# A four-stage transformer block on one core: decay exponents made by TensorE, and the last pass's mask added there

## The chip, the core and the metric

The kernel runs on one core of a Trainium2 chip. A core has five engines that run side by side, each through its own list of instructions in order: TensorE (PE in the profile; its weight loads are PEld), VectorE (DVE), ScalarE (ACT), GpSimd (POOL), and SyncE (SP), which here only issues DMAs. They wait for each other by semaphores. SBUF is the on-chip memory of 128 partitions, PSUM the accumulators that TensorE writes, in banks of 512 f32 columns. The metric is the device time of one execution in microseconds.

## The reference, cut to what matters

Input x has 128 sequences of 64 tokens of 128 values (8192 tokens), ctx the same. Four layers are applied with residuals:

```python
x = x + tanh(g_xattn[0]) * mlstm(layernorm(x), ctx, ctx, gates..., rms_scale)      # 4 heads of 32
x = x + tanh(g_ffn[0])   * switch_ffn(layernorm(x), wg, w1, b1, w2, b2)            # 8 experts, top 1
x = x + tanh(g_xattn[1]) * attention(layernorm(x), ctx, ctx, mask, W1, b1, W2, b2) # 1 head, 64x64 mask
x = x + tanh(g_ffn[1])   * (layernorm(x) @ CB.T * SCB / 127 + bias)

# mlstm, per sequence and head
cs    = concatenate([0, cumsum(log_sigmoid(fg))])
log_d = where(lower_triangle, (cs - cs.T)[1:, 1:] + ig.T, very_negative)
m     = max(log_d, axis=-1)                 # a running maximum over the tokens
d     = exp(log_d - m)                      # the decays
c     = q @ k.T / sqrt(32) * d
h     = c / (max(sum(c), exp(-m)) + eps) @ v

# attention
p     = softmax(q @ k.T / sqrt(128) + mask)
```

With a_j = ig_j - (the forget sum up to j), the exponent of a decay is a_j - M_i for j <= i and very negative otherwise, where M_i is the running maximum of a up to i.

## The kernel before, in words

The tokens are worked on in 16 groups of 512 (8 sequences; 4 tiles of 128 tokens, t = 0 to 3). The program has a first pass over the 16 groups (mLSTM, second layer norm, routing, scatter to the experts' slots in DRAM), an experts' stage (16 blocks of 512 slots), and a last pass over the 16 groups (gather, attention, last product, store).

Both passes are software pipelines written out by hand: in step k each engine does stage one of group k, stage two of group k-1, stage three of group k-2 and stage four of group k-3. `over_groups` unrolls the first and last steps and puts the middle in a loop of two steps. The order on each engine within a step is the order of calls in its `first_pass` or `last_pass`; no scheduler moves anything. In the first pass the stages are:

- one: layer norm of x, context and queries turned by PE (L889, L896), gate values from keys and queries (gate_products, L908 and L909);
- two: log of the forget gates, their sums (L915), a, turned by PE (L919), the running maxima by a scan on DVE (L1198), turned back (L923), and the decays;
- three: scores (L932), scores times decays (DVE L1210), head values (L945), RMS norm;
- four: second layer norm, turned rows (turn_routed, L953), logits (L962), the choice of an expert (DVE L1267 to L1279), the count of tokens by expert (count_tokens, L972 to L976).

The decays take this way: the scan leaves 16 rows (tile and head) of 128 maxima in SBUF (mrow). SP writes them to DRAM (spread_max, m_scratch), waits for that, and reads them back broadcast to all partitions (mb, two DMAs). POOL subtracts them from a (L619) and adds the triangle's mask (cap, L624), each over 128x1024, and ACT takes exp in SBUF (L733). The scores of all four tiles lie in the four PSUM banks of `heads`, with the head values behind them in the same banks.

A few filler products, keep_clock (L882), stand in PE's list. ACT's stage-one copy of the turned queries (L707, s_qt) is what the gate products wait for. In the last pass DVE scales the scores and adds the mask (L1408), takes the maximum (L1412) and subtracts it (L1415); then ACT takes one exp over 128x256 (L822), and PE turns the result (L1087). POOL runs the gathers (L669, four for each group) and adds a bias (L676).

## Time and profile before

| | us |
|---|---|
| median of 3 runs | 669.56 |
| lowest and highest | 668.75, 670.59 |
| the profiled execution's own time | 669.89 |
| its span, first to last instruction | 668.1 |

| engine | busy us | share of the span |
|---|---|---|
| PE | 500.9 | 75% |
| DVE | 396.4 | 59% |
| POOL | 296.6 | 44% |
| ACT | 294.6 | 44% |

The mean granted clock of TensorE is 0.771 of its full 2.4 GHz; it has two levels, 0.5 and 1.0. The first pass lasts until about 358 us, the experts' stage until about 497, and the last pass until the end. The shares are means over three stages that have different limits, so a change in one stage is to be read in that stage.

### The profile page before, as it was taken

To read this page: it belongs to the slowest core of one execution; us is meant where nothing else is said; L and a number is where in the kernel's file an instruction comes from. 1 tells how busy PE (TensorE), PEld (TensorE's weight loads), DVE (VectorE), ACT (ScalarE), POOL (GpSimd) and SP (SyncE) were. 2 spreads that over 40 slices of the span, in tenths; PEclk is the share of its full clock that TensorE was granted. 3 is DMA by queue.
4 is the path that set the end of the run, shared out by engine and by line. 5 is a ranking of instruction groups with operands and counts; after the bars stand their busy time and mean duration, and the time that the engine had idled before them with its cause. 6 is when DMAs were issued, how large, how long until landed. Compare 5 with 4: busy or idle time off the path is not lost. (4 is left out here: it accounts for less than half of the span.)

```text
span 668.1 us, 12708 instructions
## 1 busy us (share of the span) xinstructions
PE 500.9 (75%) x3659; PEld 364.5 (55%) x3659; DVE 396.4 (59%) x1536; ACT 294.6 (44%) x674; POOL 296.6 (44%) x249
## 2 busy tenths in 40 slices
PE   0637798888887888787644899999951777777685
PEld 0525676666666765566433477777740445444453
DVE  4115577777777777777662223232312699898883
ACT  3425445544444445354211333433322566666673
POOL 2024455556655555555644000000008888888720
PEclk9996657666556667556665799999995797999996
DMA  6943333222333332132501233343224445455521
GB/s 142 189 105 80 80 97 97 79 66 61 90 91 87 95 95 79 32 86 57 142 18 38 58 94 95 104 117 94 80 76 70 86 93 128 96 121 124 134 84 47
DMA packets 87362, 60.26 MB, mean 90 GB/s; under 512 B 7811, under 2 KB 79142, under 8 KB 87334
## 3 DMA queue, kind: packets, MB, share of 16 engines
q1 hardware_dynamic: 76070, 51.48, 29.5%
q0 software_dynamic: 11264, 8.43, 7.3%
q8 instruction: 14, 0.23, 0.1%
q14 instruction: 14, 0.11, 0.1%
HBM read 34.46 MB, written 17.04 MB: 77 GB/s over the span
## 5 line engine op out<-in xcount | busy, mean ns | idle before, releaser
L669 POOL DMA_INDIRECT s_xs<-slots_y,s_gidx x64 | 98.9, 1545 | 152.4 <-DMA slots_y<-s_ye 134.8
L619 POOL TENSOR_TENSOR s_ex<-s_am,s_mb 128x1024 f32<-128x1024 f32 x16 | 30.3, 1896 | 146.6 <-DMA s_mb<-m_scratch 146.6
L147 ACT ACTIVATE s_xn<-s_xs,s_ln_shift,s_ln_rstd 128x128 f32 (+1 forms) x192 | 77.6, 481 | 22.6 <-DVE s_ln_shift L140 21.8
L797 ACT ACTIVATE s_ht<-heads,s_cols 128x512 f32<-128x512 f32 x64 | 44.0, 687 | 85.2 <-PE heads L1026 84.9
L99 DVE BATCH_NORM_STATS2 s_ln_stats<-s_xs 128x6 f32 (+1 forms) x256 | 54.4, 279 | 30.7 <-DMA s_xs<-slots_y,s_gidx 19.1
L645 POOL DMA_INDIRECT slots_x<-s_xn,s_sidx x64 | 63.0, 984 | 18.2 <-issue 17.2
L1026 PE MATMUL heads<-s_xet,s_w_sb 128*128 128x512 f32 x128 | 60.5, 617 | 1.7 <-DVE s_xet L1373 1.7
L1033 PE MATMUL bank<-s_w_sb,s_ht 128*128 128x128 f32 x512 | 59.9, 275 | 0.9 <-DVE s_ye L1382 0.9
L1033 PEld LDWEIGHTS bank<-s_w_sb,s_ht 128*128 128x128 f32 x512 | 58.5, 192 | 1.5 <-issue 1.5
L932 PE MATMUL heads<-s_ht,s_kt 128*64 128x256 f32 x256 | 57.9, 602 | 0.0
L733 ACT ACTIVATE s_ex<-s_ex 128x1024 f32<-128x1024 f32 x16 | 16.9, 1057 | 80.2 <-POOL s_ex L624 80.2
L945 PE MATMUL heads<-s_vaug,s_cw 64*64 64x33 f32 x1024 | 42.8, 233 | 5.7 <-issue 5.4
L945 PEld LDWEIGHTS heads<-s_vaug,s_cw 64*64 64x64 f32 x1024 | 38.1, 149 | 13.4 <-issue 13.0
L908 PE MATMUL bank<-s_kc,s_kt 128*128 128x8 f32 x128 | 36.6, 360 | 4.5 <-ACT s_qt L707 3.9
L1382 DVE TENSOR_TENSOR s_ye<-bank,s_b2b 128x512 f32<-128x512 f32 x16 | 11.1, 692 | 47.3 <-PE bank L1033 47.3
L1373 DVE COPY s_xet<-bank 128x512 f32<-128x512 f32 x16 | 11.1, 692 | 47.1 <-PE bank L1019 47.1
L1026 PEld LDWEIGHTS heads<-s_xet,s_w_sb 128*128 128x128 f32 x128 | 24.2, 199 | 26.9 <-issue 24.3
L624 POOL TENSOR_TENSOR s_ex<-s_ex,s_cap 128x1024 f32<-128x1024 f32 x16 | 37.5, 2345 | 1.9
L716 ACT ACTIVATE s_ht<-bank 32x512 f32<-32x512 f32 x64 | 37.3, 583 | 1.2
L908 PEld LDWEIGHTS bank<-s_kc,s_kt 128*128 128x128 f32 x128 | 34.2, 328 | 6.5 <-issue 5.5
L909 PE MATMUL bank<-s_kqkv,s_qt 128*128 128x8 f32 x128 | 36.8, 361 | 0.0
L676 POOL TENSOR_TENSOR s_ex<-s_xs,s_fbias 128x512 f32<-128x512 f32 x16 | 27.4, 1711 | 19.2 <-DVE s_xs L1428 19.2
(169 smaller groups left out, 1008.7 us busy)
## 6 DMA issues: line engine op xcount, KB each, us to landing
s_mb<-m_scratch SPq DMA_DIRECT2D x32, 256.0 KB, 4.0
slots_x<-s_xe SPq DMA_DIRECT2D x8, 516.0 KB, 11.3
s_xe<-slots_x SPq DMA_DIRECT2D x16, 258.0 KB, 3.2
s_xs<-in_x_dram SPq DMA_DIRECT2D x16, 256.0 KB, 4.0
s_ctxb<-in_ctx_dram SPq DMA_DIRECT2D x16, 256.0 KB, 2.9
s_kpt<-s_kt SPq DMA_DIRECT2D x16, 256.0 KB, 4.0
s_w_sb<-in_L_ffn_w_dram SPq DMA_DIRECT2D x16, 256.0 KB, 3.2
slots_y<-s_ye SPq DMA_DIRECT2D x16, 256.0 KB, 2.3
```

The costliest lines, as they stand in the source:

```text
L99: last = dve.bn_stats(self.stats[:, i * GT + t, :], tile(t))
L147: last = act.activation(out(t), tile(t), ACT.Identity, bias=self.shift[:, j:j + 1], scale=self.rstd[:, j:j + 1])
L624: pool.tensor_tensor(ex[:, q, :].rearrange("p (r i) -> p r i", i=S), ex[:, q, :].rearrange("p (r i) -> p r i", i=S), cap[:, :].unsqueeze(1 ...
L645: pool.indirect_dma_start(out=slots_x, out_offset=bass.IndirectOffsetOnAxis(ap=sidx[:, q, t:t + 1], axis=0), in_=xn2[:, q, t, :], in_offse ...
L669: pool.indirect_dma_start(out=xs[:, n * D:(n + 1) * D], out_offset=None, in_=slots_y, in_offset=bass.IndirectOffsetOnAxis(ap=gidx[:, n:n + ...
L716: act.activation(qbd[hp, q, :].rearrange("p (b h i) -> p b h i", b=BG, h=NH)[:, :, h, :], bank[0][hp, :].rearrange("p (b i) -> p b i", b=B ...
L797: act.activation(ht[:, s_par, c, :], heads[:, c, :], ACT.Gelu_apprx_tanh, bias=col).then_inc(h_done, 1)
L908: pe.matmul(tile, kt[:, q, t * P:(t + 1) * P], kc[:, :], start=True, stop=False)
L932: last = pe.matmul(heads[(b % 2) * S:(b % 2 + 1) * S, t, 0:NH * S], kt[:, q, b * S:(b + 1) * S], qbd[:, q, b * NH * S:(b + 1) * NH * S], s ...
L945: last = pe.matmul(heads[bp, t, NH * S + h * HA:NH * S + (h + 1) * HA], cw[bp, t, h, :], vaug[bp, q, t, h, :], start=True, stop=True)
L1026: pe.matmul(heads[:, c, :], w1_sb[:, wq, c * P:(c + 1) * P], xet[:, :], start=True, stop=True).then_inc(h_ps, 1)
L1033: last = pe.matmul(bank[6][:, t * D:(t + 1) * D], ht[:, q, c, t * P:(t + 1) * P], w2_sb[:, wq, c, :], start=(c == 0), stop=(c == FC - 1))
```

## The change

Decays: mrow's two halves (the two sequences of a tile) now go straight from SBUF to two rows (partitions 32 and 33) of a right-hand tile dec_r, with two DMAs and no trip through DRAM. DVE copies the turned a to the first 16 rows of a left-hand tile dec_l. The other rows hold constants: selectors of ones for the 16 rows, -1 for the two rows of maxima, and an identity against the triangle's mask. One product of dec_l by dec_r per half, into two banks of `heads`, is the exponent, and ACT takes exp from PSUM. POOL's two passes are gone. The scores now use those two banks (two tiles each) and the head values the other two, so DVE multiplies scores by decays in two instructions in place of four, and scales the heads in one in place of four. On ACT the copy of the queries is called behind the decays and the routing's exp.

Last pass: a scaled mask is added by a product with the identity behind the scores. DVE takes the maximum from PSUM and scales it, and ACT takes exp from PSUM with the maximum as bias, in four instructions of 64 columns. POOL and DVE build the constant tiles at the start, ahead of the point at which PE and DVE begin their first pass.

```diff
             def spread_max(g, half, q):
                 hold(sp, mrow_done, g + 1, consts)
-                sp.dma_start(m_dram[q].rearrange("b (r i) -> r b i", i=S),
-                             mrow[:, q, :].rearrange("r (b i) -> r b i", b=2)).then_inc(m_out[q], 16)
-                hold(sp, m_out[q], half * 16 + 16, consts)
-                hold(sp, l_done, g - 1, consts)
+                hold(sp, l_ps, g - 1, consts)
                 for b in range(2):
-                    sp.dma_start(mb[b * S:(b + 1) * S, q, :],
-                                 m_dram[q][b:b + 1, :].to_broadcast([S, R * S])).then_inc(m_in[q], 16)
+                    sp.dma_start(dec_r[32 + b:33 + b, q, :], mrow[:, q, b * S:(b + 1) * S]).then_inc(m_in[q], 16)
...
+            pool.wait_ge(cleared, 4)
+            step(pool.memset(dec_r[0:R, :, :], 1.0))
+            for q in range(2):
+                step(pool.affine_select(out=dec_r[0:R, q, :], in_=dec_r[0:R, q, :], compare_op=ALU.is_equal, fill=0.0, base=0,
+                                        pattern=[[1, R], [0, S]], channel_multiplier=-1))
+            step(pool.tensor_copy(dec_r[S:P, :, :].rearrange("p q (r i) -> p (q r) i", i=S),
+                                  cap[S:P, :].unsqueeze(1).to_broadcast([S, 2 * R, S])))
+            step(pool.tensor_copy(dec_l[S:P, :, :].rearrange("p q (b i) -> p (q b) i", i=S),
+                                  ident[S:P, S:P].unsqueeze(1).to_broadcast([S, 4, S])))
...
-            def exponents(g, half, q):
...
-                pool.tensor_tensor(ex..., am..., mb..., ALU.subtract).then_inc(l_done, 1)
...
-                pool.tensor_tensor(ex..., ex..., cap..., ALU.add).then_inc(lcap_done, 1)
...
             def decays(g, half, q):
-                act.wait_ge(lcap_done, g + 1)
-                act.activation(ex[:, q, :], ex[:, q, :], ACT.Exp).then_inc(ex_done, 1)
+                act.wait_ge(l_ps, g + 1)
+                need(act, cw_done, nth(g - 2, 1, 2))
+                act.activation(ex[:, q, :], heads[:, 0:2, :].rearrange("p u n -> p (u n)"), ACT.Exp).then_inc(ex_done, 1)
...
                 if two:
                     values(*two)
-                if one:
-                    queries(*one)
                 if two:
                     decays(*two)
                 if four:
                     routed_exp(*four)
                 if one:
+                    queries(*one)
                     soft_part(*one)
                     queries_by_head(*one)
...
             def probabilities(g, half, q):
-                act.wait_ge(sm_steps, nth(g, 3, 3))
+                act.wait_ge(sm_steps, nth(g, 2, 2))
                 need(act, prt_ps, g)
-                act.activation(pr[:, :, :], sm[:, 1, :, :], ACT.Exp).then_inc(pr_done, 1)
+                for t in range(GT):
+                    last = act.activation(pr[:, t, :], heads[:, 0, t * S:(t + 1) * S], ACT.Exp, bias=smx[:, 1, t:t + 1],
+                                          scale=float(D) ** -0.5)
+                last.then_inc(pr_done, 1)
...
+            def decay_exponents(g, half, q):
+
+                pe.wait_ge(arow_done, g + 1)
+                hold(pe, m_in[q], half * 32 + 32, consts)
+                need(pe, cw_done, nth(g - 1, 2, 2))
+                for u in range(2):
+                    last = pe.matmul(heads[:, u, :], dec_l[:, q, :], dec_r[:, q, u * GW:(u + 1) * GW], start=True, stop=True)
+                last.then_inc(l_ps, 1)
...
             def running_max(g, half, q):
                 dve.wait_ge(at_ps, g + 1)
+                need(dve, l_ps, g - 1)
+                dve.tensor_copy(dec_l[0:R, q, :], bank[6][0:R, 128:256]).then_inc(arow_done, 1)
...
-            def exponents3(g, half, q):
+            def score_maxima(g, half, q):
...
-                dve.scalar_tensor_tensor(out=sm..., in0=heads..., scalar=float(D) ** -0.5, in1=mask..., op0=ALU.mult, op1=ALU.add)
...
+                dve.tensor_reduce(smx[:, 0, :], heads[:, 0, 0:GT * S].rearrange("p (c k) -> p c k", k=S), AX, ALU.max).then_inc(sm_steps, 1)
...
-                dve.tensor_tensor(sm..., sm..., smx..., ALU.subtract).then_inc(sm_steps, 1)
+                dve.tensor_scalar(smx[:, 1, :], smx[:, 0, :], -(float(D) ** -0.5), None, ALU.mult).then_inc(sm_steps, 1)
```

The scores of the last pass (scores3) get the product with the identity behind them:

```diff
+                pe.matmul(heads[:, 0, 0:GT * S], ident[:, :], mask_s[:, :].unsqueeze(1).to_broadcast([P, GT, S]),
+                          start=False, stop=True).then_inc(s3_ps, 1)
```

On PE, in a full step of the first pass, before, from the end of the head values to the first gate products (L953 is turn_routed, L896 turn_queries, L962 the logits, L908 and L909 the gate products):

```order
L945 MATMUL heads<-s_vaug,s_cw 64x33 x7
L953 MATMUL bank<-s_ident,s_xn 128x128 [waits ln12_applied1]
L953 MATMUL bank<-s_ident,s_xn 128x128 x3
L896 MATMUL bank<-s_ident,s_xn 128x128 [waits qbd_done,ln12_applied0]
L896 MATMUL bank<-s_ident,s_xn 128x128 x3
L962 MATMUL bank<-s_wg_sb,s_xt 128x8 [waits xt2_done,late_in]
L962 MATMUL bank<-s_wg_sb,s_xt 128x8 x3
L908 MATMUL bank<-s_kc,s_kt 128x8 [waits qt_done,mtok_done,kt_done]
```

The same place now (L961 is turn_routed, L928 the new product, L893 turn_queries, L970 the logits, L905 the first gate product):

```order
L961 MATMUL bank<-s_ident,s_xn 128x128 [waits cum_used]
L961 MATMUL bank<-s_ident,s_xn 128x128 x3
L37 ISA [waits arow_done]
L928 MATMUL heads<-s_dec_r,s_dec_l 128x512 [waits cw_done,m_in1,consts]
L928 MATMUL heads<-s_dec_r,s_dec_l 128x512
L890 REGISTER_ALU
L29 REGISTER_ALU [waits ln12_applied0]
L893 MATMUL bank<-s_ident,s_xn 128x128 [waits qbd_done]
L893 MATMUL bank<-s_ident,s_xn 128x128 x3
L970 MATMUL bank<-s_wg_sb,s_xt 128x8 [waits xt2_done]
L970 MATMUL bank<-s_wg_sb,s_xt 128x8 x3
L905 MATMUL bank<-s_kc,s_kt 128x8 [waits mtok_done,qt_done,consts,kt_done]
```

Two 128x512 products have come between the turned rows and the turned queries; the order around them is as it was.

On ACT, in a full step, before, from the copy of the values (L702) to the four copies of the queries by head (L716):

```order
L702 ACTIVATE s_vaug<-s_ctxb 128x16x32 [waits pv_done]
L707 ACTIVATE s_qt<-bank 128x512 [waits xt1_done]
L733 ACTIVATE s_ex<-s_ex 128x1024 [waits lcap_done]
L753 ISA
L29 ISA [waits route]
L755 ACTIVATE s_spread<-s_below 128x32 [waits weight_done]
L721 ISA
L722 ACTIVATE s_eneg<-s_negabs 128x16 [waits gate_steps]
L723 ISA
L724 ACTIVATE s_softp<-s_eneg 128x16 [waits gate_act]
L716 ACTIVATE s_ht<-bank 32x8x64 x4
```

The same place now (L696 copies the values, L728 is the decays' exp, L750 the routing's, L701 the queries' copy):

```order
L696 ACTIVATE s_vaug<-s_ctxb 128x16x32 [waits pv_done]
L29 ISA [waits l_ps]
L728 ACTIVATE s_ex<-heads 128x1024 [waits cw_done]
L748 ISA
L29 ISA [waits route]
L750 ACTIVATE s_spread<-s_below 128x32 [waits weight_done]
L701 ACTIVATE s_qt<-bank 128x512 [waits xt1_done]
L715 ISA
L716 ACTIVATE s_eneg<-s_negabs 128x16 [waits gate_steps]
L717 ISA
L718 ACTIVATE s_softp<-s_eneg 128x16 [waits gate_act]
L710 ACTIVATE s_ht<-bank 32x8x64 x4
```

The copy of the queries has moved from ahead of the decays' exp to behind the routing's.

## Rows read from the trace of the kernel before

**Rows 1.** Busy time by window: start:end and length, each engine, clock, DMA.

```profile
core 0: us, PE busy (x) PEld busy (x) DVE busy (x) ACT busy (x) POOL busy (x), PEclk, DMA share, GB/s
60.00:318.00 258.00, 219.34 (x1707) 167.17 (x1708) 190.61 (x765) 122.61 (x293) 143.37 (x119) 0.62 0.28 78
376.00:499.00 123.00, 116.95 (x695) 86.42 (x693) 34.57 (x62) 43.88 (x63) 0.00 (x0) 1.00 0.32 88
```

**Rows 2.** Waits: who for whom, us in total, times, longest.

```profile
PE bank L972 <- DVE s_onehot L1279: 18.7, 15, 3.5
```

**Rows 3.** Timeline of one step: start us, us, engine line, operation [idle before].

```profile
167.60 0.69 PE L953 MATMUL bank<-s_ident,s_xn 128*128 128x128 f32 x4 [1.23 <-DVE s_xn L154]
...
169.20 1.85 PE L962 MATMUL bank<-s_wg_sb,s_xt 128*128 128x8 f32 x8
...
170.56 0.58 ACT L707 ACTIVATE s_qt<-bank 128x512 f32<-128x512 f32 x1
...
171.29 0.56 PE L908 MATMUL bank<-s_kc,s_kt 128*128 128x8 f32 x2 [0.23 <-ACT s_qt L707]
...
173.35 2.34 POOL L624 TENSOR_TENSOR s_ex<-s_ex,s_cap 128x1024 f32<-128x1024 f32 x1
...
173.60 2.13 DVE L1279 TENSOR_TENSOR s_onehot<-s_first_best,s_choice 128x32 bf16<-128x32 f32 x1
...
174.26 0.57 PE L909 MATMUL bank<-s_kqkv,s_qt 128*128 128x8 f32 x2
...
175.80 0.21 PE L972 MATMUL bank<-s_onehot,s_tri_b 128*128 128x40 bf16 x1 [0.96 <-DVE s_onehot L1279]
...
176.60 1.98 PE L932 MATMUL heads<-s_ht,s_kt 128*64 128x256 f32 x8
```

**Rows 4.** Busy time by window, three short stretches of that step.

```profile
160.11:161.08 0.97, 0.97 (x7) 0.74 (x8) 0.85 (x4) 0.95 (x2) 0.67 (x2) 0.50 0.18 64
...
162.05:163.02 0.97, 0.97 (x21) 0.75 (x20) 0.81 (x9) 0.00 (x0) 0.86 (x1) 1.00 0.20 68
...
168.84:169.81 0.97, 0.97 (x6) 0.80 (x5) 0.70 (x2) 0.49 (x2) 0.00 (x0) 0.50 0.93 224
```

**Rows 5.** Timeline of the experts' stage, L1026 at its start and later.

```profile
370.78 6.41 PE L1026 MATMUL heads<-s_xet,s_w_sb 128*128 128x512 f32 x8 [0.94 <-DVE s_xet L1373]
...
400.85 3.60 PE L1026 MATMUL heads<-s_xet,s_w_sb 128*128 128x512 f32 x8
```

**Rows 6.** The scan in the timeline; the page's DMA issues, last number us to landing.

```profile
163.78 0.41 DVE L1198 TENSOR_TENSOR_SCAN s_mrow<-s_reset,bank 16x128 f32<-16x128 f32 x1 [0.76 <-PE bank L919]
...
s_mb<-m_scratch SPq DMA_DIRECT2D x32, 256.0 KB, 4.0
```

**Rows 7.** Timeline of the last step of the first pass, logits to exponential.

```profile
354.05 1.87 PE L962 MATMUL bank<-s_wg_sb,s_xt 128*128 128x8 f32 x8 [0.69 <-ACT s_xt L750]
...
356.41 0.23 ACT L755 ACTIVATE s_spread<-s_below 128x32 f32<-128x32 f32 x1 [2.42 <-DVE s_below L1270]
```

**Rows 8.** Timeline, PE: a wait for logf, and the last three waits for onehot.

```profile
83.81 0.61 PE L915 MATMUL bank<-s_logf,s_tri 128*128 128x16 f32 x2 [2.12 <-DVE s_logf L1184]
...
330.75 0.22 PE L972 MATMUL bank<-s_onehot,s_tri_b 128*128 128x40 bf16 x1 [3.39 <-DVE s_onehot L1279]
...
346.91 0.21 PE L972 MATMUL bank<-s_onehot,s_tri_b 128*128 128x40 bf16 x1 [2.99 <-DVE s_onehot L1279]
...
357.11 0.21 PE L972 MATMUL bank<-s_onehot,s_tri_b 128*128 128x40 bf16 x1 [1.19 <-DVE s_onehot L1279]
```

**Rows 9.** Timeline of the start.

```profile
6.41 1.11 PE L889 MATMUL bank<-s_ident,s_ctxb 128*128 128x128 f32 x4 [6.41 <-POOL s_carry L611]
...
12.54 0.86 DVE L99 BATCH_NORM_STATS2 s_ln_stats<-s_xs 128x6 f32<-128x128 f32 x4
...
31.16 0.59 SPq L465 DMA_DIRECT2D m_scratch<-s_mrow  x1
...
47.95 0.61 PE L915 MATMUL bank<-s_logf,s_tri 128*128 128x16 f32 x2 [10.31 <-DVE s_logf L1184]
```

**Rows 10.** Last pass: a wait of POOL's, and DVE's masked scores (count, busy, mean ns).

```profile
POOL s_ex L676 <- DVE s_xs L1428: 19.2, 4, 5.9
...
L1408 DVE SCALAR_TENSOR_TENSOR s_sm<-heads,s_mask 128x256 f32<-128x256 f32 x14 | 5.9, 424 | 5.1 <-PE heads L1078 4.9
```

More of the change, by code:

```diff
@@ L188, in sem @@
             return ctx.enter_context(nc.semaphore(name))
-        m_dram = [nc.dram_tensor(f"m_scratch{i}", (2, R * S), F32, kind="Internal").ap() for i in range(2)]
         slots_x = nc.dram_tensor("slots_x", (E * N, D + 1), F32, kind="Internal").ap()
@@ L341, in flamingo @@
         mrow_done = sem("mrow_done")
-        m_out = [sem(f"m_out{i}") for i in range(2)]
         m_in = [sem(f"m_in{i}") for i in range(2)]
@@ L648, in first_pass @@
             def first_pass(at):
-                _, two, three, _, five = at
+                _, _, three, _, five = at
                 if five:
                     scatter(*five)
-                if two:
-                    exponents(*two)
                 if three:
@@ L938, in head_values @@
                 for t in tiles_of:
-                    hold(pe, cw_done, nth(g, t + 1, GT), consts)
+                    if t % 2 == 0:
+                        hold(pe, cw_done, nth(g, t // 2 + 1, 2), consts)
                     if t == 0:
                         pe.wait_ge(vaug_done, g + 1)
+                        need(pe, hs_done, g)
                     for h in range(NH):
@@ L1001, in first_pass @@
                     turn_routed(*four)
+                if two:
+                    decay_exponents(*two)
                 if one:
@@ L1074, in scores3 @@
                 pe.wait_ge(kpr_in[q], half * 16 + 16)
-                need(pe, sm_steps, nth(g - 1, 1, 3))
+                need(pe, pr_done, g)
                 for b in range(BG):
                     u, p, c = b // 4, b // 2 % 2, b % 2
-                    last = pe.matmul(heads[p * S:(p + 1) * S, 0, (2 * u + c) * S:(2 * u + c + 1) * S],
-                                     qp[:, q, b * S:(b + 1) * S], kpr[:, q, b * S:(b + 1) * S], start=True, stop=True)
-                last.then_inc(s3_ps, 1)
+                    pe.matmul(heads[p * S:(p + 1) * S, 0, (2 * u + c) * S:(2 * u + c + 1) * S],
+                              qp[:, q, b * S:(b + 1) * S], kpr[:, q, b * S:(b + 1) * S], start=(u == 0 and c == 0), stop=False)
+                if isinstance(g, int) and g == 0:
+                    pe.wait_ge(mask_done, 1)
+                pe.matmul(heads[:, 0, 0:GT * S], ident[:, :], mask_s[:, :].unsqueeze(1).to_broadcast([P, GT, S]),
+                          start=False, stop=True).then_inc(s3_ps, 1)
             def turn_probabilities(g, half, q):
@@ L1326, in first_pass @@
                 if three:
-                    decayed_scores(three[0], three[2], (0, 1))
+                    decayed_scores(three[0], three[2], 0)
                 if two:
@@ L1338, in first_pass @@
                 if three:
-                    decayed_scores(three[0], three[2], (2, 3))
+                    decayed_scores(three[0], three[2], 1)
                 if two:
@@ L1462, in last_pass @@
                 if three:
-                    exponents3(*three)
+                    score_maxima(*three)
                 if four:
```

91 lines of the change are left out of this document (41 added, 50 removed).

## The prediction, made before the changed kernel ran

> **What bounds the kernel now.** I read the stages first, in a table of busy time by window [rows 1]: the reader should see that in the first pass (60 to 318 us) PE is busy 219.3 of 258 us at a mean granted clock of 0.62, with DVE at 191 and POOL at 143. So the first pass belongs to PE, at mostly half clock, while the experts' stage runs at full clock. Then the waits of PE's count of tokens for DVE's onehot, 18.7 us in 15 waits [rows 2], and then one turn of the loop in order of time [rows 3]: PE goes almost without a pause from the turned rows (L953, 167.60) over the logits (L962, 169.20) and the gate products (sixteen instructions, L908 at 171.29 to L909 at 174.26, which ends at 174.83). Then it stands until 175.80, because DVE's 32-column onehot (L1279) takes 2.13 us: it ends at 175.73, just after POOL's 2.34 us L624 (175.69). PE's order is fixed, so what is put into it is paid in full unless it fills one of these pauses. The clock in the step goes 0.50, 1.00, 0.50 [rows 4]: it rises once the scores and the filler products have run and falls again under the narrow products.
>
> **Product on PE (two 128x512 f32).** Each becomes two instructions, and stands between L953 and L896 in the order. At half clock four such calls (x8) take 6.4 us from 370.78, the last of them already after the rise, and L1026 at full clock has x8 in 3.60 [rows 5]. At 1.2 GHz a call streams four times 512 columns, 1.7 us, so the pair costs 3.4 us; at 2.4 GHz 1.8. Its place, 168.3, is at 0.50 [rows 4], so 3.4 is the upper end. But 3.4 us of wide streaming resembles what stands ahead of the rise in the trace, so I expect the granted clock to rise behind it for a short while. There lie the logits (1.85) and the gate products (3.5); they are many weight loads and gain some 40%, not 50%. I take 1.2 us back, net 2.2. The lower end is 1.0 (part of the product at full clock, and the return).
>
> Is its input there? The scan of the maxima ends at 164.19, and the copy put ahead of it on DVE adds 0.2. The old broadcast took 4.0 us from issue to landing, the new transfers of 4 KB less; even with 4.0 the rows are in by 168.7 against 168.3 [rows 6]. The cost is 0 to 0.4; I take 0.1 with the copy.
>
> **The queries' copy on ACT moves behind routed_exp.** Now ACT copies the queries (L707, 0.58) at 170.56, while PE does the logits, and the gate products begin 0.24 behind the logits' end (171.05, 171.29) [rows 3]. In the new order the copy stands behind the exponential of the routing (routed_exp), which waits for DVE's first two steps on the logits. In an undisturbed place that chain is seen alone: logits end 355.92, exponential 356.41 to 356.64, so 0.72 [rows 7]. Add the copy, 0.6 with handoff, and 0.15 to PE: 1.47, less the 0.24 of now: **1.25 us more on PE in each step that has both**. Nothing lies between logits and gate products in PE's order to hide it. Zero would need the logits to be done long before, which the order excludes; 1.6 if DVE or ACT is late. Also queued behind that copy is soft_part, but it waits for the gate products anyway.
>
> **POOL's two passes over 128x1024 go.** They hold up DVE. With them gone the onehot is ready during the gate products, whose later start covers it. Of 18.7 us of waits [rows 2] the last three (3.39, 2.99, 1.19) belong to the drained end of the pass [rows 8]; 11.1 are left in 12 full steps and go. Once PE also waited 2.12 us for logf [rows 8], behind a late exponent; that goes. add_heads remains on POOL, earlier in the step, and can still stall DVE, under cover of the gate products. SP's DRAM round trip was not awaited in the middle of the pass, and its loss gives nothing more. Fewer and longer DVE instructions on PSUM and fewer waits at the head values lie in DVE's slack: 0.
>
> **Start.** POOL now builds wide constant tiles (6,144 columns in four instructions and some small ones) behind two more clears on DVE. By L624's 2.34 us for 1024 columns that is 14 us; one-input work should be cheaper, I take 10. The last constant, now at 6.4, then comes at 20 (16 to 25), and DVE's first statistics start there instead of at 12.54 [rows 9]. But SP sends the first maxima only at 31.16, behind its clearing of the slots, and PE's next forget_sums stands until 47.95 with 10.31 us of waiting [rows 9]. The delay of 8 us goes almost wholly into that wait: maxima at 34, landed at 37, product to 41, queries and gate products to 46, forget_sums at 48.6. I take +1.6 for the first two groups; ends 0 and +8.
>
> **Last pass.** The mask's product adds two instructions of 256 columns, 0.45 us at full clock; the DVE add (0.42) and the subtract over 128x256 go, a tiny multiply comes; four small exponentials replace one on ACT, about 0.7 more. While POOL gathers, it sets the pace: it waits for DVE in only 4 of its adds [rows 10]. So nothing there, and about +1 over the last steps, where ACT and PE are in the chain (-1 to +3).
>
> **Sum**, by the profiled run, 669.9 us with its surroundings for a span of 668.1, 0.3 above the median of 669.56:
> - 12 full steps x (2.2 + 1.25 + 0.1) = +42.6
> - waits that go, -11.1 - 2.1 = -13.2
> - one filling step without the stall: 3.5; start 1.6; drained end: product 3.2 against 2.2 of the 3.39: +1.0. Together +6.1
> - last pass +1.0
>
> In all +36.5, so 706.4 by the profiled run and **706 us** by the median. With the product at its lower end: 12.5 x 1.2 = 15 less, 691; at its upper end 15 more, 721.
>
> **Rivals.**
> 1. *The clock stays up through the pass, and the kernel is faster.* For it: in the experts' stage, with wide products all along, the clock is 1.00 [rows 1], and the new product comes where it is lowest. Against it: some 7 us of narrow products follow it, and the clock now falls in just such a stretch. Price: half clock covers about 11 us of PE work per step, which would give back 4.8; against the product's 1.8, 1.25 and 0.1, less 1.0 of waits, the step is 2.6 us shorter; over 12.5 steps -32, about 640. It decides from the point where the clock gives back 2.9 us per step beyond my 1.2 (36.5 over 12.5 steps). The Trainium skill, TensorE: Matmul & The Clock Gate (What's actually happening), says that the throttled state is the default and activity releases it. By that rule more activity can only help, and it speaks for this rival; by the trace the release does not last a step, which speaks for 706.
> 2. *The product is paid in full at 1.2 GHz* and the start is partly bare: 12.5 x 1.2 + 4 more, 725. For it: the product begins at 0.50 every time in the trace. Against: the rise behind each wide stretch.
> 3. *The product comes nearly free of clock cost*, the rise falls within it: about 691.
> 4. *PE isn't the bound, the stalls are.* The product would lie in the present waits: -13 and some 14 for the copy and the start, about 669, no change. Against it: PE's wait ahead of L953 is upstream of the product, and behind it only the onehot's wait is left.
>
> **Chances.** Forecast (697 to 715) 0.60; rival 3 and what lies near it, 0.15; rival 2, 0.12; rival 1, 0.07; rival 4, 0.06. A measurement of this kernel tells 0.3%, 2 us, from no change. Faster: rival 1 and a third of rival 4, 0.09; within: 0.03; slower 0.88. The range 687 to 722 leaves out rivals 1 and 4 and the far end of 2.
>
> **What would show it.** The pair of 128x512 products should take 3.4 us where the clock starts at 0.50, with a rise behind it. The first gate product should stand 1.4 us idle behind ACT's copy of the queries; count of tokens should no longer wait for the onehot, and that instruction should be 0.2 us. The step should be 21.5 to 22 us against about 19 now. The first statistics on DVE should start near 20 us, and forget_sums of the second group near 48.6. In the last pass POOL's gathers should keep their spacing. I am wrong if the mean clock of the first pass is well above 0.7, or if PE idles elsewhere and the step stays near 19.

## The result: slightly faster, where 5.5% slower was forecast

The changed kernel takes 665.26 us (median of 12 runs, 656.54 to 673.09), the kernel before 669.15 (12 runs beside them, 666.05 to 673.66). The ratio is 0.9883, 95% interval 0.9847 to 0.9919. In two later sets of runs, each beside the kernel before, it was 0.9732 (0.9682 to 0.9781) and 0.9649 (0.9582 to 0.9716). The forecast was 706, with 687 as the lower end, so it was wrong in sign. Ratios leave out executions over 1.5% above the fastest of their kernel and medians do not; below, ratios are compared.

The profiled execution took 669.75 us with a span of 668.0, at a mean granted clock of 0.830 (before: 669.89, 668.1 and 0.771). As it is one of the longer executions of the changed kernel, it shows mostly the long kind of step, and an execution with a span of 646.8 us stands beside it further down.

Busy time by window in the profile after (columns as in [rows 1]): the first pass, and its 12 full steps alone.

```profile
60.00:318.00 258.00, 214.78 (x1722) 151.06 (x1722) 152.45 (x695) 119.42 (x286) 82.38 (x87) 0.74 0.16 51
82.31:320.50 238.19, 197.08 (x1597) 138.60 (x1596) 143.18 (x648) 110.21 (x264) 79.99 (x84) 0.74 0.16 51
```

Against [rows 1] POOL's busy time fell from 143 to 82 us, DVE's from 191 to 152, and PE's from 219 to 215 although two wide products per step were added: the granted clock rose from 0.62 to 0.74. The mean full step is 19.85 us, forecast at 21.5 to 22 and 19.57 before.

What PE waited for from 60 to 318 us (us in total, times, longest us):

```profile
PE bank L905 <- ACT s_qt L701: 18.1, 13, 1.5
PE bank L961 <- DVE s_xn L154: 16.0, 13, 1.5
```

The wait for the onehot [rows 2] is gone from the full steps. The one that was forecast in its place, of the gate products for the queries' copy, has come with 1.4 us each. One step in order of time answers to [rows 3] (start us, us, engine line, operation, idle before):

```profile
175.32 0.65 PE L961 MATMUL bank<-s_ident,s_xn 128*128 128x128 f32 x4 [1.34 <-DVE s_xn L154]
175.81 1.88 PE L928 MATMUL heads<-s_dec_r,s_dec_l 128*128 128x512 f32 x4
177.52 0.60 PE L893 MATMUL bank<-s_ident,s_xn 128*128 128x128 f32 x4
177.96 0.96 PE L970 MATMUL bank<-s_wg_sb,s_xt 128*128 128x8 f32 x8
...
179.06 0.18 DVE L1282 TENSOR_REDUCE s_top<-bank 128x4 f32<-128x32 f32 x1
...
179.59 0.23 ACT L750 ACTIVATE s_spread<-s_below 128x32 f32<-128x32 f32 x1 [0.29 <-DVE s_below L1285]
179.72 0.58 ACT L701 ACTIVATE s_qt<-bank 128x512 f32<-128x512 f32 x1
180.44 0.36 PE L905 MATMUL bank<-s_kc,s_kt 128*128 128x8 f32 x2 [1.53 <-ACT s_qt L701]
...
180.96 1.16 DVE L1294 TENSOR_TENSOR s_onehot<-s_first_best,s_choice 128x32 bf16<-128x32 f32 x1
...
183.44 0.19 PE L980 MATMUL bank<-s_onehot,s_tri_b 128*128 128x40 bf16 x1
```

Read this against the forecast. The four product instructions take 1.88 us, because the clock is up here; the forecast had it down. Behind them the logits take 0.96 instead of 1.85 us. The logits end at 178.92, but DVE takes the first look at them only at 179.06, as it was still scaling the heads; then the exponential, the copy and the gate products follow, 1.52 us behind the logits. The count (183.44) no longer waits. This is one of the three full steps of the profile in which the product takes 1.88 us (18.89 us long); in the other nine it takes 3.0 to 3.6.

The start came as forecast (timeline, start us, us, engine line, operation; answers to [rows 9]):

```profile
19.25 1.12 PE L886 MATMUL bank<-s_ident,s_ctxb 128*128 128x128 f32 x4 [19.25 <-POOL s_carry L621]
...
33.13 1.25 SPq L467 DMA_DIRECT2D s_dec_r<-s_mrow  x2
...
48.30 0.45 PE L912 MATMUL bank<-s_logf,s_tri 128*128 128x16 f32 x2
```

Forecast were 20, 34 and 48.6. The first full step of the loop began at 82.31 against 78.75. The last gather of the last pass started at 632.32 against 628.40, and the last output's work at 664.50 against 664.67, so the end is 4.1 us shorter. That distance varies from one execution to the next, though: it is 32.2 us here, 34.9 in a later profile of the changed kernel, 36.3 before and 34.6 in another profile with the last pass as before.

### The profile page after: what moved, and what is told of

The parts are those of the page before. It is cut to its first block and busy times, and to the rows that moved or that the text cites. A ratio compares the mean times of both kernels' runs of the same rounds, so it can differ in the third digit from the quotient of the medians.

```text
span 668.0 us, 12750 instructions
## 1 busy us (share of the span) xinstructions
PE 508.3 (76%) x3755; PEld 353.9 (53%) x3755; DVE 349.0 (52%) x1459; ACT 301.2 (45%) x722; POOL 238.0 (36%) x225
## 5 line engine op out<-in xcount | busy, mean ns | idle before, releaser
L627 POOL TENSOR_TENSOR s_hs<-s_hs,s_head_w 128x512 f32<-128x512 f32 x16 | 20.2, 1264 | 154.4 <-DVE s_hs L1268 154.4
L928 PE MATMUL heads<-s_dec_r,s_dec_l 128*128 128x512 f32 x64 | 49.9, 927 | 5.3 <-DMA s_dec_r<-s_mrow 4.7
L953 PE MATMUL heads<-s_vaug,s_cw 64*64 64x33 f32 x1024 | 39.6, 226 | 9.1 <-issue 6.9
L905 PE MATMUL bank<-s_kc,s_kt 128*128 128x8 f32 x128 | 29.9, 306 | 21.7 <-ACT s_qt L701 21.7
L953 PEld LDWEIGHTS heads<-s_vaug,s_cw 64*64 64x64 f32 x1024 | 36.1, 141 | 15.9 <-issue 15.4
L905 PEld LDWEIGHTS bank<-s_kc,s_kt 128*128 128x128 f32 x128 | 26.6, 257 | 23.3 <-issue 23.3
L1397 DVE TENSOR_TENSOR s_ye<-bank,s_b2b 128x512 f32<-128x512 f32 x16 | 11.1, 691 | 47.3 <-PE bank L1043 47.3
L716 ACT ACTIVATE s_eneg<-s_negabs 128x16 f32<-128x16 f32 x16 | 3.5, 216 | 71.1 <-DVE s_negabs L1193 71.1
L1388 DVE COPY s_xet<-bank 128x512 f32<-128x512 f32 x16 | 11.1, 692 | 46.0 <-PE bank L1029 46.0
L1073 PE MATMUL bank<-s_ident,s_xn 128*128 128x128 f32 x64 | 11.4, 304 | 29.8 <-ACT s_xn L147 29.8
L118 ACT ACTIVATE s_ln_log<-s_ln_ve 128x8 f32<-128x8 f32 (+1 forms) x38 | 7.7, 204 | 56.6 <-DVE s_ln_ve L112 51.3
```

What stands on the lines that cost most here:

```text
L905: pe.matmul(tile, kt[:, q, t * P:(t + 1) * P], kc[:, :], start=True, stop=False)
L928: last = pe.matmul(heads[:, u, :], dec_l[:, q, :], dec_r[:, q, u * GW:(u + 1) * GW], start=True, stop=True)
L953: last = pe.matmul(heads[bp, 2 + t // 2, (t % 2 * NH + h) * HA:(t % 2 * NH + h + 1) * HA], cw[bp, t, h, :], vaug[bp, q, t, h, :], start=Tr ...
```

## The experiments

Ratios are to the kernel before, with its 95% interval; a change "on queries first" starts from the first kernel.

**Parts of the change.** First, the changed kernel with ScalarE's copy of the queries ahead of the decays' exponential, as it was, in two sets of runs:

```diff
+                if one:
+                    queries(*one)
                 if two:
                     decays(*two)
                 if four:
                     routed_exp(*four)
                 if one:
-                    queries(*one)
                     soft_part(*one)
```

> The changed kernel with ACT's copy of the queries called ahead of the decays' exp again. If that copy, waiting behind the routing's exp, costs PE 1.25 us per step as forecast (1.36 measured as L905's wait), the wait goes and the kernel gains 12 x 1.2 = 14 us against the changed one: about 0.967 of the kernel before. Rival: the pause is only moved, since the logits and the choice then hold up the count of tokens, or the clock falls sooner: within 4 us of the changed kernel, 0.985 to 0.995.

> ScalarE's copy of the queries ahead of the decays' exponential, as before. Its 1.36 us per step alone would give 12 x 1.36 = 16 us under the changed kernel of this batch. If it also brings all the steps to the kind with the product at full clock, the gain is over 16 us and no step of the profile is near 20 us.

Measured: 631.47 us, 0.9523 (0.9485 to 0.9562), and again 631.02 us, 0.9523 (0.9481 to 0.9564). In the second set the changed kernel stood at 0.9649, so the copy's place costs 0.0126, 8 us, with an interval of some 5 us to either side; by the medians (645.97) it is 15. Other readings are higher: against the changed kernel's 0.9732 in its other set it is 14 us, and by the mean full step (17.03 us here, 18.10 and 18.19 in the two later profiles of the changed kernel) 13 to 14. The forecast's 15 is at the upper end of that. My expectation for the first set, 0.967 from the result's ratio, was too cautious. My expectation that no step would be near 20 held (16.28 to 17.85).

Decays and order as changed, last pass as before (the functions probabilities, scores3 and exponents3 of the kernel before put back):

> The decays' half of the change alone, the last pass as before. Theory: the first pass is 4 to 6 us later in its end, and the last pass (4 us shorter after the last gather in the changed kernel) gets its time back: 0.995 to 1.005. Rival: the gain of 4 us in the last pass came with the phase of the clock and not with the edit: the same as the changed kernel, about 0.988.

Measured: 651.24 us, 0.9812 (0.9763 to 0.9861), faster than either of my two expectations. It differs from queries first in the copy's place and in the last pass; in this set the two together are 0.0289, 19 us. The last pass's half alone:

> The last pass's half alone, the decays as before. Theory: DVE has 0.4 to 0.7 us less per step there, it is no longer a step behind POOL's gathers, and the kernel gains about 4 us: 0.994. The forecast's term: +1 us, 1.0015. Rival: phase of the clock, 1.000.

Measured: 660.37 us, 0.9973 (0.994 to 1.0005), which is -1.8 us (-4.0 to +0.3). The last output's work started 34.8 us behind the last gather's start, within the 34.6 to 36.3 of the profiles with the last pass as before. Forecast was +1.0; whether this half gains anything is not shown.

The kernel before with the new constants, built into tiles that nothing reads (CONSTS 29, the same memsets and selects):

> The kernel before with the changed kernel's eight more constants and two more clears, built into tiles that nothing reads. The forecast's term for the start: +1.6 us (ends 0 and +8), 1.002 of the kernel before. With the whole delay of DVE's first statistics on the path, +7 us, 1.010.

Measured: 662.75 us, 0.9998 (0.9974 to 1.0022). The first full step began at 82.11, as in the changed kernel, and yet nothing of that is left at the end. Its mean full step is 19.06 us (19.57 in the profile before), so it also serves as a second profile of the old order.

The kernel before with one POOL pass over 128x1024 instead of two:

```diff
                 pool.tensor_tensor(ex...,
-                                   am[:, q, :].unsqueeze(2).to_broadcast([P, R, S]),
+                                   cap[:, :].unsqueeze(1).to_broadcast([P, R, S]),
                                    mb..., ALU.subtract).then_inc(l_done, 1)
...
-                pool.tensor_tensor(ex..., ex..., cap..., ALU.add).then_inc(lcap_done, 1)
...
-                act.wait_ge(lcap_done, g + 1)
+                act.wait_ge(l_done, g + 1)
```

> The kernel before, where POOL makes the exponents in one pass over 128x1024 instead of two (cap less maxima; the gates' part is left out, so the exponents are not the reference's). By the forecast's term, the wait of the count for DVE's onehot goes: 0.93 us in each of 12 full steps, 11 us less, 0.983 of the kernel before. If the stall of DVE by POOL costs nothing else, and the clock stands as before, no more than that. If the clock is what sets the step, 0.99 to 1.00.

Measured: 641.41 us, 0.9676 (0.9646 to 0.9705), 21 us less, where the forecast had 13.2 for both passes. What PE waited for over the 12 full steps (us in total, times, longest), first before, then with one pass:

```profile
PE bank L972 <- DVE s_onehot L1279: 11.1, 12, 3.5
PE bank L915 <- DVE s_logf L1184: 2.1, 1, 2.1
```

```profile
PE bank L968 <- DVE s_onehot L1275: 3.2, 8, 0.5
PE bank L911 <- DVE s_logf L1180: 0.4, 1, 0.4
```

DVE's three small instructions with two inputs from SBUF, over the same steps (groups, busy us and mean ns), first before, then with one pass:

```profile
L1279 DVE TENSOR_TENSOR s_onehot<-s_first_best,s_choice 128x32 bf16<-128x32 f32 x12 | 24.5, 2043 | 0.4
L1273 DVE SCALAR_TENSOR_TENSOR s_first_best<-s_below,s_prio 128x32 f32<-128x32 f32 x12 | 12.3, 1023 | 0.4
L1178 DVE SCALAR_TENSOR_TENSOR s_negabs<-s_gates 128x16 f32<-128x16 f32 x12 | 9.9, 822 | 0.4
```

```profile
L1269 DVE SCALAR_TENSOR_TENSOR s_first_best<-s_below,s_prio 128x32 f32<-128x32 f32 x12 | 17.9, 1495 | 0.4
L1275 DVE TENSOR_TENSOR s_onehot<-s_first_best,s_choice 128x32 bf16<-128x32 f32 x12 | 12.2, 1014 | 0.4
L1174 DVE SCALAR_TENSOR_TENSOR s_negabs<-s_gates 128x16 f32<-128x16 f32 x12 | 4.7, 391 | 0.4
```

Together the three fall from 3.89 to 2.90 us per step. The third is the first step of the gates; it stood beside POOL's add_heads, which ran late because it comes behind the two passes.

The wait for the onehot that is gone, 7.9 us, is less than half of the gain: the step falls from 19.57 us (19.06 in the profile with the constants) to 17.39. The rest can be read against the profile with the constants, 20 us over the 12 steps. PE stands idle 10.0 us less (36.6 to 26.6). There PE waited 8.4 us in 4 steps for DVE's logf, in a chain of lateness: POOL's second pass ends at 103.53, ACT's exponential of the decays at 104.62, the routing's exponential behind it at 104.73, and only then DVE goes on to the gates (104.77) and logf. With one pass 0.4 us of that wait is left. These waits are about 0.7 of the 1.1 us by which the turned rows begin earlier in the step (9.07 instead of 10.18). The other 10.2 us are PE's own busy time (192.2 to 182.0 for the same instructions), at a granted clock of 0.67 instead of 0.63. Whether the clock rose because the stalls went, or the step is shorter because the clock rose, this run does not tell.

**The product.** Made twice in the changed kernel (`for u in (0, 1, 0, 1)`):

> The changed kernel with the pair of products issued twice. Forecast's price: another 2.2 to 3.4 us per step, 1.03 of before. By the clock theory the second pair runs at full clock (1.7 us) and lengthens the rise: 0.2 to 1.5 us per step, 0.99 to 1.01.

Measured: 682.63 us in 3 rounds (669.59 to 684.47) against 645.84 for the changed kernel beside it, that is +37 us by the medians. Of its four executions three took 682.19 to 684.47 us and one 669.59, only 24 above. In the profile (683.07) each step is 20.3 to 20.6 us, 2.3 more in the mean than the changed kernel's 18.19 in that set. DVE now stands in every step until the logits are done, while in the changed kernel's execution with a span of 646.8 us, shown below, it did so for 4.7 us in 3 steps (us in total, times, longest):

```profile
DVE s_top L1282 <- PE bank L970: 37.1, 12, 3.1
```

The changed kernel in that set:

> The changed kernel again, beside the next three on the same chip. Expected 0.985 to 0.992 of the kernel before, with steps of two kinds in the first pass: about 17.5 us where the wide product runs at full clock (1.7 us from its start to the turned queries' less 0.1) and about 20.3 us where it runs at half clock (2.8 us and more). The spread between executions is then the share of the two kinds.

Measured: 645.84 us, 0.9732 (0.9682 to 0.9781). Now the other way, a quarter of the product's columns (768 of 1,024 left out):

```diff
-                act.activation(ex..., heads[:, 0:2, :]..., ACT.Exp).then_inc(ex_done, 1)
+                act.activation(ex..., heads[:, 0:2, 0:128].unsqueeze(2).to_broadcast([P, 2, 4, 128]), ACT.Exp).then_inc(ex_done, 1)
...
-                    last = pe.matmul(heads[:, u, :], dec_l[:, q, :], dec_r[:, q, u * GW:(u + 1) * GW], ...)
+                    last = pe.matmul(heads[:, u, 0:128], dec_l[:, q, :], dec_r[:, q, u * GW:u * GW + 128], ...)
```

> The changed kernel with only 128 of each 512 columns of the product made; ScalarE reads them four times over, so its exponential keeps its length (three quarters of the exponents are those of other groups and heads). TensorE streams 1024 columns per step less at four passes: 2.6 us at half clock, 1.3 at full. If PE's work is what counts, each of the 12 full steps is 1.3 to 2.6 us shorter than in the changed kernel: 16 to 30 us less in all, some 625 to 635 where the changed kernel takes 650. If the wide product pays for itself through the clock, the logits and the gate products behind it go back to 0.50 and the time stays within 8 us of the changed kernel, or goes above it.

> The changed kernel once more, on the chip of its neighbours in this batch. 0.970 to 0.99 of the kernel before. If the step comes in two kinds (product at full clock, about 17.5 us; product begun at half clock, about 20.3 us), the profile shows both or one of them, and no length between.

Measured: 641.82 us, 0.9696 (0.9651 to 0.9741), and for the changed kernel beside it 645.97 us, 0.9649 (0.9582 to 0.9716). Three quarters of the product gone, and nothing is gained. Busy time by window over the 12 full steps, the changed kernel and then the quarter product:

```profile
81.46:298.67 217.21, 186.64 (x1598) 135.34 (x1597) 148.93 (x648) 109.64 (x264) 79.75 (x84) 0.77 0.18 56
```

```profile
81.28:293.14 211.86, 171.26 (x1598) 130.77 (x1597) 152.49 (x648) 108.86 (x264) 79.83 (x84) 0.77 0.19 58
```

PE is busy 1.3 us per step less at the same clock of 0.77, so it is not the clock that takes the gain back. The mean step is 17.65 us against 18.10, but only because the three long steps are missing: the nine others of the changed kernel have a mean of 17.2. The expectation on the lengths of the changed kernel's steps was too neat: they are 16.1 to 18.1 us in nine cases and 20.1, 21.3 and 21.3 in three. Two places of that execution on PE (timeline), a short step and a long one, and then the short step with a quarter product:

```profile
196.70 0.65 PE L961 MATMUL bank<-s_ident,s_xn 128*128 128x128 f32 x4 [0.74 <-DVE s_xn L154]
197.19 1.88 PE L928 MATMUL heads<-s_dec_r,s_dec_l 128*128 128x512 f32 x4
198.91 0.60 PE L893 MATMUL bank<-s_ident,s_xn 128*128 128x128 f32 x4
199.35 0.96 PE L970 MATMUL bank<-s_wg_sb,s_xt 128*128 128x8 f32 x8
201.82 0.36 PE L905 MATMUL bank<-s_kc,s_kt 128*128 128x8 f32 x2 [1.52 <-ACT s_qt L701]
...
232.46 1.11 PE L961 MATMUL bank<-s_ident,s_xn 128*128 128x128 f32 x4 [0.29 <-DVE s_xn L154]
233.37 3.31 PE L928 MATMUL heads<-s_dec_r,s_dec_l 128*128 128x512 f32 x4
```

```profile
196.25 0.65 PE L961 MATMUL bank<-s_ident,s_xn 128*128 128x128 f32 x4 [0.86 <-DVE s_xn L154]
196.74 0.61 PE L928 MATMUL heads<-s_dec_r,s_dec_l 128*128 128x128 f32 x4
197.19 0.60 PE L893 MATMUL bank<-s_ident,s_xn 128*128 128x128 f32 x4
197.84 1.06 PE L970 MATMUL bank<-s_wg_sb,s_xt 128*128 128x8 f32 x8
201.38 0.36 PE L905 MATMUL bank<-s_kc,s_kt 128*128 128x8 f32 x2 [2.48 <-ACT s_qt L701]
```

From the turned rows to the gate products it is 5.12 us in the short step with the whole product and 5.13 with a quarter. What the product no longer takes goes into the wait for the copy (1.52 to 2.48), because the copy stands behind DVE's chain (squares, heads, first look at the logits), which didn't move. The long step begins with the turned rows at half clock (1.11 instead of 0.65) and has the product in 3.31, as forecast at half clock. From the rows to the gate products it then takes 6.5 to 6.9 us, and DVE waits for the logits: in such a step the product is no longer hidden. The longer executions have more of them: products of 2.9 us and more are 9 of 12 in the profile after, 4 of 12 in the changed kernel's second profile and 3 of 12 here, at spans of 668.0, 644.2 and 646.8. In the profile after, DVE's waits for the logits come to 15.6 us in 9 steps.

The same quarter on queries first, where no copy is waited for:

> Queries first, with 128 of each 512 columns of the product made (exponents of the wrong groups). Here the gate products don't wait for ScalarE, so the product's 1.3 us (full clock) or 2.6 (half) are bare. If PE's work is what counts, 12 x 1.3 to 2.6 = 15 to 31 us less than queries first: 0.905 to 0.93 of the kernel before. If the clock or DVE's onehot takes it back, within 6 us of queries first (0.952): 0.943 to 0.96.

Measured: 633.95 us, 0.9567 (0.9533 to 0.96), not below the 0.9523 with the whole product. This pair is less clear than the one above, since here the clock did fall (0.78 to 0.70, lines further down): the rows, the quarter product and what follows run at half clock in nearly every step, and from the turned rows to the gate products it is 3.7 us, as in the short steps with the whole product.

**Wide filler work into the pauses.** Eight bf16 products of 512 columns ahead of the turned queries, in the kernel before:

> The kernel before with eight more filler products (bf16, 128x512) ahead of the turned queries, in the new product's place, 3.4 us at half clock. If wide streaming there raises the clock for what follows, as in the changed kernel where 3.0 us of product cost only about 0.5 net, the step grows by at most 1 us: 1.00 to 1.02. If the clock gives nothing back, 12.5 x 3.4 = 42 us: 1.06.

Measured: 658.89 us, 0.9955 (0.9926 to 0.9983). In its profile the turned queries begin 2.2 us (full clock) or 3.7 (half) behind the turned rows, instead of 0.9, in every step, and the kernel is slightly faster. Busy time by window over the 12 full steps, before and with the filler, and then PE's wait for the onehot with it (11.1 us before):

```profile
78.75:313.65 234.90, 197.84 (x1550) 151.44 (x1549) 175.50 (x696) 111.01 (x265) 132.07 (x110) 0.62 0.29 79
82.37:305.84 223.47, 182.11 (x1646) 125.96 (x1645) 175.16 (x696) 110.44 (x265) 129.50 (x109) 0.75 0.30 83
...
PE bank L973 <- DVE s_onehot L1280: 27.1, 12, 3.1
```

With more work PE was busy less, as the clock rose: 15.7 us less, or 10.1 less than in the profile with the constants (192.2). Against that profile the 12 steps are 5.3 us shorter, and the other 4.8 us are idle time of PE, with its wait for DVE's onehot at 2.3 us per step. So in the kernel before PE's time set the step only in part. Five ahead of the gate products of the changed kernel (keep_clock(1, 5)):

> The changed kernel with five wide bf16 products (512 columns each) in TensorE's wait for the copy of the queries, just ahead of the gate products. They cost 1.1 us at full clock, 2.1 at half, in a pause of 1.5. If half clock under the gate products is what makes the step long, these run at full clock (1.9 us instead of 3.1 to 3.4) and the step is up to 1.2 us shorter: 5 to 14 us under the changed kernel, 0.945 to 0.96 of the kernel before. If the gate products don't matter because the count of tokens then waits for DVE's onehot, 0 to 3 us less; if the filler is paid, 6 us more.

Measured: 638.9 us, 0.9652 (0.9613 to 0.969). The gate products do run at full clock then (0.37 a pair instead of 0.57 mostly), but the step is 17.85 us against 18.10, and the ratio is that of the changed kernel in its last set (0.9649). My larger term fell. In this profile the product runs at half clock for most of its length in all 12 full steps (2.9 us or more until the turned queries), and nine of the steps are still 16.9 to 17.6 us long. A slow product alone does not make a long step. The product in one of them, 17.6 us long:

```profile
121.64 3.20 PE L929 MATMUL heads<-s_dec_r,s_dec_l 128*128 128x512 f32 x4
```

Three ahead of the gate products, and, in another kernel, four ahead of the turned rows, both on queries first:

> The one above with 3 wide bf16 products of 512 columns ahead of the gate products, in the pause of TensorE of about 1 us that is left there. Costs 0.65 us of stream at full clock, 1.3 at half, against a pause of 0.7 to 1.05: 0 to 0.5 us more per step if the clock is up there anyway (0 to +6 us against the one above). If the clock falls in that pause, the gate products win up to 1.7 us and the kernel is 5 to 15 us faster than the one above.

> Queries first, and four wide bf16 products ahead of the turned rows, in TensorE's pause of 0.8 to 1.3 us for DVE's normalised rows. Cost 0.9 us at full clock, inside that pause. If the steps with the product at half clock come from the pause ahead of it, all the steps are of the kind with the product at 1.72 us, and the mean step goes from 16.9 to 16.6 or less: 3 to 8 us under queries first, 0.94 to 0.948. If not, 0.952 to 0.957.

Measured: 629.85 us, 0.9508 (0.9466 to 0.955), and 632.38 us, 0.9527 (0.9485 to 0.9569): no difference from queries first. In the second the product took 1.72 us until the turned queries in each of the 12 full steps, as expected, and the mean step stayed at 17.00. Busy time by window over the 12 full steps, three kernels: queries first, the same with a quarter product, and with the filler ahead of the turned rows.

```profile
78.93:283.24 204.31, 181.67 (x1598) 125.55 (x1597) 148.68 (x648) 108.34 (x264) 79.90 (x84) 0.78 0.19 60
```

```profile
79.71:284.78 205.07, 178.72 (x1597) 137.79 (x1597) 153.40 (x648) 108.67 (x264) 79.83 (x84) 0.70 0.19 60
```

```profile
79.40:283.39 203.99, 185.99 (x1645) 126.46 (x1645) 153.42 (x648) 107.23 (x264) 79.82 (x84) 0.80 0.19 60
```

The clock goes from 0.70 to 0.80 and PE's busy time from 14.9 to 15.5 us a step, while the step is 17.03, 17.09 and 17.00 us. What PE is busy less, it waits more. Something else holds the step there. With the quarter product, PE waits for the onehot in each full step and DVE waits for PE's count (waits, us in total, times, longest):

```profile
PE bank L981 <- DVE s_onehot L1295: 14.5, 12, 1.3
```

```profile
DVE s_own L1303 <- PE bank L985: 11.7, 12, 1.0
DVE s_ss L1246 <- ACT s_sq L732: 8.6, 12, 0.7
DVE s_zz L1255 <- ACT s_zz L741: 6.4, 12, 0.5
DVE s_dec_l L1213 <- PE bank L917: 6.3, 12, 0.6
```

These are handoffs of half a microsecond to one, once a step, in a ring: onehot, count on PE, own place on DVE, all of DVE's list, onehot. DVE is busy 12.8 us of a step, and these four handoffs are 2.75 more; the rest up to 17.1 are two smaller waits (0.5) and short gaps between dependent instructions. In the changed kernel the ring takes another way, over DVE's first look at the logits, ACT's exponential and copy, and the gate products to the count; there DVE waits 25.9 us in 12 steps for the count (execution with a span of 646.8 us). In the last instructions of the ring DVE still runs beside POOL's add_heads (timeline of that kernel):

```profile
110.19 1.26 POOL L627 TENSOR_TENSOR s_hs<-s_hs,s_head_w 128x512 f32<-128x512 f32 x1 [6.99 <-DVE s_hs L1269]
...
110.57 0.93 DVE L1289 SCALAR_TENSOR_TENSOR s_first_best<-s_below,s_prio 128x32 f32<-128x32 f32 x1
...
111.53 1.26 POOL L630 TENSOR_TENSOR s_xs<-s_xs,s_hs 128x512 f32<-128x512 f32 x1
111.64 0.19 DVE L1293 TENSOR_REDUCE s_choice<-s_first_best 128x32 f32 x1
111.86 0.98 DVE L1295 TENSOR_TENSOR s_onehot<-s_first_best,s_choice 128x32 bf16<-128x32 f32 x1
```

The instruction of 32 columns with one input takes 0.19 us, those with two inputs from SBUF 0.93 and 0.98. The Trainium skill, SBUF — State Buffer (SBUF: two separate sides), says that DVE and GpSimd take one pair of ports in turn, each for a whole instruction, and that a DVE instruction with two SBUF inputs meets it against a GpSimd one that reads SBUF. The trace agrees: the two-input instructions end at 111.50 and 112.84, each 0.05 us behind the end of POOL's (111.45 and 112.79), and the one-input instruction, which starts beside POOL's second, is not held.

## Why the prediction was wrong, step by step

| step of the forecast | forecast | measured |
|---|---|---|
| product, net of the clock's return, 12 steps | +26.4 us | nothing beside a quarter of it (0.9649 whole, 0.9696 a quarter, same clock); partly paid in the steps where it runs at half clock |
| queries' copy behind the routing, 12 steps | +15 | +8 (3 to 14) by the ratios of one set, 13 to 15 by the others and by the steps |
| waits that go | -13.2 | -21 for one of POOL's two passes alone; 7.9 of it PE's wait for the onehot |
| start | +1.6 (0 to 8) | 0 (-1.7 to +1.5) |
| last pass | +1.0 (-1 to +3) | -1.8 (-4.0 to +0.3) |
| copy and rows for the product; filling step and drained end | +1.2; +4.5 | not tried alone |
| sum | +36.5 | -8 to -23 by set of runs |

**The step that failed** is in the first part: "PE's order is fixed, so what is put into it is paid in full unless it fills one of these pauses", and with it "net 2.2". The order is fixed, but PE alone did not set the length of the step. I read its busy 219 of 258 us [rows 1] as the bound, and the wait for the onehot as a pause of PE. It is the sign of a ring through DVE. Where PE waits for DVE in every step and DVE for PE's count, work put on PE between two such waits is paid only once it is longer than the wait behind it. At full clock the first product is not: three quarters of it taken away, 1.3 us of PE's busy time per step, gained nothing. At half clock it is in part, and the second product is in every step: made twice it costs 24 to 37 us, 2.3 us per step in the profile. In the kernel before PE's time set the step in part: with the fillers PE was busy 10.1 us less, and about half of that came off the steps.

**The price of the product** itself was right at both clocks: 3.0 to 3.6 us in the long steps (forecast 3.4) and 1.72 to 1.88 in the short ones (forecast 1.8). That "the product begins at 0.50 every time in the trace" (rival 2) was carried over from the kernel before and was false: in most steps of two of three profiles it begins at full clock. The logits behind it fell to 0.96 from 1.85.

**The copy of the queries** was the part that was read best: 1.47 behind the logits was forecast, 1.52 came, and undoing it was worth 8 to 15 us, against the 15 of the forecast.

**The waits that go** were undersized. I priced POOL's passes by PE's waits for the onehot, 11.1 us, and by one wait for logf, 2.1. One pass away gives 21 us. It takes 7.9 us off the waits for the onehot; the waits for logf, of which the profile before happened to have one and another profile of the same order four (8.4 us), are a term that I had too small, and the higher clock during the same instructions is one that I did not have. I also left out a third DVE instruction that POOL held up (L1178, 0.82 us in the mean before, 0.175 in the changed kernel), because PE was not seen to wait for it. A stall in a ring is paid in the ring, not only where the other engine is seen to wait. That DVE would have slack once its instructions were fewer ("DVE's slack: 0") was the same mistake. The onehot fell to a mean of 0.43 us in the profile after, not to 0.2; in the step shown above it takes 1.16, beside add_heads.

**Start and last pass**: every point of the start was met (19.25, 33.13, 48.30; POOL waits 4.9 us for DVE's clears and works 7.9 on the constants, where I took 10 for the work), and the 3.4 us that it moves the loop are not in the end time. The last pass was forecast at +1.0 (-1 to +3) and measured at -1.8 (-4.0 to +0.3), just outside these bounds and not clear of nothing.

**Rivals.** Rival 4 (PE is not the bound, the stalls are: about 669) was nearest, and had a chance of 0.06. I set it aside because "behind it only the onehot's wait is left"; that wait was the evidence for it. Its number is close in part by luck: it took -13 for the waits and nothing for the product, where one POOL pass alone measured -21 and the product is partly paid in the long steps. Rival 1 (clock) had the sign right and the mechanism only in part: the clock of the first pass rose to 0.74, and to 0.77 in the two other profiles, above the 0.7 that I named as the mark of an error. But with queries first 0.70 and 0.80 go with the same step.

**What stays open.** The separate pieces sum to about -21 + 8 - 2 = -15 us (-8 with 15 for the copy) for the changed kernel, within what the sets of runs show; the second POOL pass away was not tried alone. How much of that pass's 21 us comes by the clock is not settled. Nor is what puts one execution of the changed kernel mostly into long steps and another mostly into short ones. It is what their times differ by: 21 of the 21 us between the spans of 668.0 and 646.8 lie in the 12 full steps. In the two later profiles the long steps begin with PE at half clock at the turned rows, but with the fillers ahead of the gate products steps that begin so are short.

**The better kernel** is the changed one with the queries' copy left where it was: 631.0 us, 0.9523 of the kernel before, and below the changed kernel. The wide fillers on top of it add nothing that can be told.

## What to carry to other kernels

An engine with 85% busy time need not be the bound if it waits once a step for an engine that in turn waits once a step for it: add the ring (busy time of the other engine's list and the handoffs) and compare it with the step before pricing work as paid in full. A cheap test is to change the work of the engine that is taken for the bound and to read its busy time and clock with it. The quarter product did this cleanly, 1.3 us less per step at the same clock; the fillers did not, since they raised the clock and made PE's busy time shorter, not longer. And when a change moves one call behind another on an engine, try it without the move, since here it took back a quarter of the gain or more.

## What the runs showed of the hardware that I had not expected

- POOL's passes of 1.90 and 2.34 us over 128x1024 f32, and its add_heads of 1.26, held up three DVE instructions of 16 or 32 columns with two SBUF inputs, to 0.82, 1.02 and 2.04 us in the mean. The first of them takes 0.175 us in the changed kernel. Taking one pass from each step gave 1.8 us per step, although the three became only 1.0 us shorter together.
- Filler products can be free or better in a mixed loop: 0.9955 (0.9926 to 0.9983) with eight per step, as PE's busy time fell by 10 to 16 us while the granted clock went from 0.62 to 0.75.
- The changed kernel runs with steps of 16.1 to 21.3 us side by side in one execution. There the long ones are those whose 128x512 f32 pair takes 2.9 us or more instead of 1.88, but with five fillers per step pairs of that length stood in steps of 16.9 to 17.6 us too.
